# Router logits in column halves, weight splits in half-size pieces moved into the expert loop, and 24 unread TensorE products ahead of the attention

## The reference

```python
x = x + 0.5 * _L0_ffn_ref(_layernorm(x), router_w, w1, v1, w2)
x = x + _L0_attn_ref(_layernorm(x), Wq, bq, Wk, bk, Wv, bv, Wo, bo)
x = x + 0.5 * _L0_ffn_ref(_layernorm(x), router_w, w1, v1, w2)
```

## Time and profile before

| | us |
|---|---|
| median of 3 runs | 712.66 (712.17 to 713.16) |
| the profiled execution | 714.14 |
| span, first to last instruction, of that execution | 712.3 |
| busy: PE / PEld / DVE / ACT / POOL | 624.0 / 525.3 / 518.4 / 373.0 / 52.6 |
| mean granted TensorE clock | 0.950 of full |

### The profile page before, as it was taken

One profiled execution on the slowest core, in us unless ns is written; L12 is line 12 of the kernel. 1 busy time (PEld: TensorE's weight loads), 2 busy tenths in 40 slices (PEclk: granted clock), 3 DMA queues, 4 the chain that ended last, 5 costly groups with the idle time before them and its releaser, 6 DMA issues.

```text
span 712.3 us, 11934 instructions
## 1 busy us (share of the span) xinstructions
PE 624.0 (88%) x4498; PEld 525.3 (74%) x4498; DVE 518.4 (73%) x1308; ACT 373.0 (52%) x1001; POOL 52.6 (7%) x55
## 2 busy tenths in 40 slices
PE   3627985899999999999999999999999998663996
PEld 1414764699998979999897999898899996331775
DVE  6773656889987777878777777876878776865543
ACT  1403453576656656666555656565556665231432
POOL 3134300000000000000000000000000000115310
PEclk9956996999999999999999999999999999896999
DMA  8994970000000000000000000000000052793481
GB/s 328 407 351 153 373 277 1 0 1 1 1 1 2 1 1 1 1 1 1 1 1 1 1 1 1 1 1 0 1 1 1 1 204 93 311 397 87 156 300 46
DMA packets 27229, 62.50 MB, mean 88 GB/s; under 512 B 6880, under 2 KB 17248, under 8 KB 26912
## 3 DMA queue, kind: packets, MB, share of 16 engines
q1 hardware_dynamic: 25152, 56.05, 20.8%
q0 software_dynamic: 1568, 5.25, 2.2%
q10 hardware_dynamic: 448, 0.39, 0.2%
HBM read 54.34 MB, written 7.34 MB: 87 GB/s over the span
## 4 chain that ended last, share of the span: by engine, by line
PE 80%; DVE 11%; ACT 5%; DMA 2%; issue 1%; POOL 0%; SPq 0%; DVEq 0%; ACTq 0%
PE bank L1183 19%; PE bank L1185 18%; PE bank L1184 18%; PE bank L1235 8%; PE bank L1042 4%; PE bank L1074 4%; PE bank L1084 2%; PE bank L1117 2%; PE bank L1013 2%; DVE best L773 1%; DVE ln L695 1%; DMA slots<-token_table,slot_index 1%; PE bank L1026 1%; DVE keys L775 1%; DVE stats L683 1%
## 5 line engine op out<-in xcount | busy, mean ns | idle before, releaser
L609 ACT ACTIVATE probs<-bank,negmax 128x256 f32<-128x256 f32 x256 | 121.4, 494 | 0.0
L622 ACT CAST probsT_hi<-bank 128x512 fp32r<-128x512 f32 x128 | 68.8, 590 | 79.7 <-PE bank L1235 79.7
L957 DVE TENSOR_TENSOR probsT_lo<-bank,probsT_hi 128x512 fp32r<-128x512 f32 x128 | 81.8, 681 | 0.8 <-ACT probsT_hi L622 0.8
L925 DVE TENSOR_REDUCE negmax<-bank 128x2 f32<-128x512 f32 x128 | 81.8, 680 | 0.5 <-PE bank L1185 0.5
L592 ACT ACTIVATE o_hi<-bank,bv 128x512 fp32r<-128x512 f32 x64 | 44.2, 690 | 64.6 <-PE bank L1185 64.6
L1183 PE MATMUL bank<-k_hi,q_hi 128*128 128x256 f32 x256 | 72.5, 283 | 2.7 <-DVE q_lo L911 2.7
L933 DVE TENSOR_SCALAR probs<-probs,rowinv 128x256 f32<-128x256 f32 x256 | 73.1, 349 | 2.3
L1183 PE MATMUL bank<-o_hi,wo_hi 128*128 128x256 f32 x256 | 73.1, 286 | 1.6 <-DVE o_lo L911 1.6
L911 DVE SCALAR_TENSOR_TENSOR o_lo<-bank,bv,o_hi 128x512 fp32r<-128x512 f32 x64 | 48.0, 750 | 36.1 <-ACT o_hi L592 36.1
L1185 PE MATMUL bank<-o_hi,wo_lo 128*128 128x256 f32 x256 | 72.5, 283 | 0.0
L1185 PE MATMUL bank<-k_hi,q_lo 128*128 128x256 f32 x256 | 72.4, 283 | 0.0
(11 more groups left out here) (162 smaller groups left out, 1321.7 us busy)
## 6 DMA issues: line engine op xcount, KB each, us to landing
up_r<-up_in SPq DMA_DIRECT2D x16, 768.0 KB, 8.9
down_r<-down_in SPq DMA_DIRECT2D x14, 512.0 KB, 10.4
up_q<-up_in SPq DMA_DIRECT2D x8, 768.0 KB, 8.8
up_o<-up_in SPq DMA_DIRECT2D x6, 768.0 KB, 12.6
down_q<-down_in SPq DMA_DIRECT2D x8, 512.0 KB, 9.9
token_table<-xn SPq DMA_DIRECT2D x16, 256.0 KB, 10.7
down_o<-down_in SPq DMA_DIRECT2D x6, 512.0 KB, 14.2
x<-x_in SPq DMA_DIRECT2D x4, 512.0 KB, 5.4
```

The lines of the kernel that those rows point to most:

```text
L609: nc.scalar.activation(probs[:, n % 2, t, :], scores_ps[head][:, qt * S:qt * S + S], ACT.Exp, bias=negmax[:, n % 2, t:t + 1], accum_out=ro ...
L622: nc.scalar.copy(probsT[0][:, head].rearrange("p c s -> p (c s)"), probsT_ps[head][:]).then_inc(probsT_high, 1)
L925: nc.vector.reduce_max(negmax[:, n % 2, 2 * head:2 * head + 2], scores_ps[head][:].rearrange("p (t s) -> p t s", t=2), AX.X, negate=True). ...
L957: nc.vector.tensor_tensor(probsT[1][:, head].rearrange("p c s -> p (c s)"), probsT_ps[head][:], probsT[0][:, head].rearrange("p c s -> p ( ...
```

## The change

The router's product of four tiles is written as four products of 64 output rows and 256 columns, in which the two pairs of tiles use the two column halves of the array (`experts_of`); its result is 128 rows by 256 columns, so that it is copied and transposed back in two pieces instead of four. PE transposes up to three pairs ahead. At the start all 16 tiles are normalised together. The moment chain is grouped in 13 levels, within which operations don't wait for each other. The splits become 20 pieces of 512 columns; six of them move into steps 9 to 15 of layer 0's slot loop. SP holds the loads of groups 8 to 11 until three gathers have landed. The means of the first tiles are read from PSUM, and ACT does all four copies into `x`. In layer 1 POOL makes its keys after the last normalised tile. Two small stores at the end move from ACT's queue to POOL's, and one wide store from SP's to ACT's. PE runs 20 float32 products of 128 columns after layer 0's last sums, and 4 after the first transposes of the attention.

```diff
@@ sync: loads and stores @@
-            for g in range(6, 10):
+            for g in range(6, 8):
                 load(0, g)
             store_weights()
-            for g in range(10, AHEAD):
+            for n in range(3):
+                sp.wait_ge(gathered[n], 16)
+            for g in range(8, AHEAD):
                 load(0, g)
...
@@ gpsimd @@
             def expert_layer(layer):
+                if layer == 1:
+                    pool.wait_ge(xn_ready, 2 * TILES)
...
             expert_layer(1)
+            pool.wait_ge(staged[2], 1)
+            for j in range(2, 4):
+                store_narrow(nc.gpsimd, j, narrow_stored)
+            pool.wait_ge(narrow_stored, 32)
@@ scalar @@
+                if layer == 0 and SPLIT_AT <= s < SPLIT_AT + V_SPLIT:
+                    split_high(s - SPLIT_AT)
...
+                for u in range(3):
+                    copy_tokens(u)
+                for n in range(3):
+                    copy_expert_major(n)
+                    copy_tokens(2 * n + 3)
+                    if n > 0:
+                        copy_logits(n - 1)
+                    if n < 2:
+                        copy_tokens(2 * n + 4)
+                copy_expert_major(3)
+                copy_logits(2)
                 copy_logits(3)
...
-            for n in range(2):
+            for n, seen in ((1, (bank_summed, 2)), (0, (first_sums_read, 1))):
+                act.wait_ge(*seen)
+                for odd in range(2):
+                    nc.scalar.copy(rows_of_bank(n, odd), bank[6 + n][WIDE * odd:WIDE * odd + WIDE, :].rearrange(
+                        "p (b d) -> p b d", b=2)).then_inc(x_final, 1)
+            for n in range(6, 8):
                 split_high(n)
-            act.wait_ge(bank_summed, 2)
...
             warm(ACT.Exp)
-            split_high(3)
+            for n in range(8, 12):
+                split_high(n)
             act.wait_ge(bq_scaled, 1)
@@ vector @@
+                def level(*ops):
+                    dve.wait_ge(link, linked.now())
+                    for op, *args in ops:
+                        last = op(*args)
+                    last.then_inc(link, 1)
+                    linked.add()
...
+                    if layer == 0 and SPLIT_AT < s <= SPLIT_AT + V_SPLIT:
+                        split_low(s - SPLIT_AT - 1)
...
-                    split_low(0)
                     dve.wait_ge(bank_summed, 1)
                     for odd in range(2):
-                        nc.vector.tensor_copy(x[0:WIDE, 2 * odd, :], bank[6][WIDE * odd:WIDE * odd + WIDE, 0:D]).then_inc(x_final, 1)
+                        last = nc.vector.bn_stats(stats[0:WIDE, 2 * odd, :], bank[6][WIDE * odd:WIDE * odd + WIDE, 0:D])
+                    last.then_inc(first_sums_read, 1)
...
-            for n in range(2):
-                for m in range(2):
-                    dve.wait_ge(x_loaded[2 * n + m], 16)
-                    last = spread(range(8 * n + 4 * m, 8 * n + 4 * m + 4))
-                tie(last)
-                moments(8 * n, 8 * n + 8)
-                normalise(8 * n, 8 * n + 8)
+            for n in range(4):
+                dve.wait_ge(x_loaded[n], 16)
+                last = spread(range(4 * n, 4 * n + 4))
+            tie(last)
+            moments(0, TILES)
+            normalise(0, TILES)
...
+            in_fill = {2: 6, 3: 7, 5: 8, 7: 9}
+            in_step = {n: [lambda n=n: split_low(n + 9)] for n in range(1, 9)}
+            for n in range(2, 7):
+                in_step[n].append(lambda n=n: spread_first(2 * n))
+            in_step[7].append(lambda: tie(spread_first(14)))
+            in_step[8] += late_moments[:6]
+            in_step.update({9: late_moments[6:], 10: [lambda: split_low(18)], 11: [lambda: split_low(19)]})
@@ tensor @@
+            def keep_busy(count):
+                for _ in range(count):
+                    mm(bank[3][:, 0:KD * E], ident[:], router_w[:].rearrange("p k e -> p (k e)"),
+                       start=True, stop=True)
...
+                def experts_of(n):
+
+                    pe.wait_ge(xnT_ready, 8 * layer + 2 * n + 2)
+                    for kd in range(KD):
+                        for pair in range(2):
+                            last = mm(bank[3 + n % 2][E * pair:E * pair + E, 0:2 * P], router_w[:, kd, :],
+                                      xnT[:, (2 * n + pair) % 4, :, kd, :], start=kd == 0, stop=kd == KD - 1,
+                                      tile_position=(0, E * pair))
+                    last.then_inc(logitsT_raw, 1)
...
+                for u in range(3):
+                    transpose_tokens(u)
+                for n in range(4):
+                    experts_of(n)
+                    if n < 3:
+                        transpose_tokens(2 * n + 3)
+                    if n > 0:
+                        logits_of(n - 1)
+                    if n < 2:
+                        transpose_tokens(2 * n + 4)
                 logits_of(3)
...
+                if layer == 0:
+                    keep_busy(20)
                 pe.wait_ge(limit_ready, layer + 1)
...
             for n, job in enumerate(first_fills):
+                if n == KD:
+                    keep_busy(4)
```

More of the change, by code:

```diff
@@ L147, in macaron_kernel @@
                 exp8 = sb(router, "exp8", [P, TILES, 8])
-                key_i32 = sb(router, "key_i32", [P, T // 2], i32)
+                with ExitStack() as lent:
+                    sb(lent, "place_of_key_of_column", [P, T // 2])
+                    key_i32 = sb(lent, "key_i32", [P, T // 2], i32)
                 key_of_column = sb(router, "key_of_column", [P, T // 2])
@@ L426, in _ @@
             sp.wait_ge(staged[1], 1)
-            for odd in range(2):
-                store_wide(sp, 1, odd)
-            sp.wait_ge(out_stored, 16 * 10)
+            store_wide(sp, 1, 0)
+            sp.wait_ge(out_stored, 16 * 8)
         @block.gpsimd
@@ L559, in expert_layer @@
                         store_wide(nc.scalar, 0, odd)
-                    act.wait_ge(staged[2], 1)
-                    for j in range(2, 4):
-                        store_narrow(nc.scalar, j)
+                    act.wait_ge(staged[1], 1)
+                    store_wide(nc.scalar, 1, 1)
             def split_high(n):
@@ L650, in _ @@
                 for n in range(1, STEPS + 1):
-                    if i == 0 and n + 5 < len(splits):
-                        split_high(n + 5)
+                    if i == 0 and n + 11 < len(splits):
+                        split_high(n + 11)
                     step(n)
@@ L849, in late_range @@
                 dve.wait_ge(late_added[layer], r + 1)
-                if layer == 0 and r > 1:
-                    spread(range(1, TILES, 2))
+                if layer == 0:
+                    for a in range(0, TILES, 2):
+                        last = nc.vector.bn_stats(stats[WIDE:P, a, :], x[WIDE:P, a, :]) if r == 1 else spread([a + 1])
+                    last.then_inc(late_spread, 1)
+                    dve.wait_ge(late_spread, r)
             def split_low(n):
@@ L983, in _ @@
                     normalise_probs(0)
-                if between:
-                    between.pop(0)()
+                if n in in_fill:
+                    split_low(in_fill[n])
             step(0)
```

144 lines of the change are left out of this document (54 added, 90 removed).

## The result

The changed kernel takes 707.55 us in the median of 5 executions (705.54 to 710.26); the kernel before takes 712.85 beside it (712.17 to 714.06). The ratio is 0.9924, 95% interval 0.9907 to 0.9941: faster by 0.8%, but by 5.3 us and not by 17.7. The profiled execution is the slowest of the five: 710.26, span 708.4, which is 3.9 under the span before.

The account below looks back on a forecast made before the run. TensorE at full speed bounds the attention's middle; gains lie where it waits, in routers, gathers and the passage. Terms -2.7 - 4.85 + 0.3 - 5.05 + 0.4 - 5.2 - 0.6 = -17.7 gave 695.0 us, range 691 to 700.5.

Parts of the forecast that it names:

- Layer 0's router: Start of layer 0: with column halves side by side, POOL's subtraction starts earlier than its old 32.60; -2.7 us.
- rival 4: Routers of both layers: the product's halves don't run side by side, layer 0 gains nothing; 698 us, chance 8%.
- Layer 0's gather: Layer 0, slot numbers to first slots: weights' store lands early and no loads run beside the gather; -4.85 us.
- the slot loop: Layer 0's slots: the splits moved there are covered by engine gaps by less than 0.1 a slot; +0.3 us.
- Rival 6: Layer 0's slots: SP's hold makes weights late for ScalarE's split, so the kernel is slower; 716 us, chance 2%.
- The passage: Layer 0's last sums to the attention's second scores: earlier first fill (-2.35) and later gains (2.7); -5.05 us in all.
- rival 3: Passage to the attention: unread products stand in the way or the clock falls anyway; 698 to 699 us, chance 13%.
- First block: Attention's first block: VectorE ends 1.4 late in step 9, against TensorE slack of about 1; +0.4 us.
- Layer 1: Layer 1's router and gather: slot numbers 6.1 earlier, but the gather waits for the weights' store near 644.2; -5.2 us.
- Layer 1's slots: Layer 1, from first slots to the last stage copy: no change forecast, 0 us.
- The end: Last stores: all of SP's and ACT's issued by 709.1, POOL's two end no later; -0.6 us.
- Rival 2: Gathers of both layers gain only half, held by descriptors rather than loads; 700 us, chance 13%.

Follow-up runs that it names:

- e1: The changed kernel with SP holding layer 0's loads 8 to 11 for the first gather only, not three: 706.23 us, ratio 0.9922 to the kernel before.
- e5: The changed kernel with wq's later columns (1.5 of 2 MB) loaded behind group 15: 703.83 us, ratio 0.9872 to the kernel before.
- e4: The changed kernel without the 20 unread products after layer 0's last sums: 705.69 us, ratio 0.9904 to the kernel before.
- e10: The combined kernel e9 without the 20 unread products: 700.39 us, ratio 0.9821 to the kernel before.
- e3: The changed kernel with the end's narrow stores back on ACT's queue and the last wide one on SP's: 705.06 us, ratio 0.9877 to the kernel before.
- e9: The changed kernel with the edits of e5, e8 and e3 together: 699.94 us, ratio 0.9826 to the kernel before.
- e7: The changed kernel with layer 1's loads of groups 8 to 11 behind the token and weight stores, without a hold: 707.26 us, ratio 0.9934 to the kernel before.
- e8: The changed kernel with layer 1's loads of groups 8 to 11 behind the stores and held for three gathers: 704.27 us, ratio 0.9879 to the kernel before.

## Why the prediction was wrong, step by step

**Layer 0's router: right.** -2.99 at POOL's start, -2.7 forecast; rival 4 is out.

**Layer 0's gather: right at its place, and lost behind it.** First slots -7.83 for -7.55. The step that failed is the end of that paragraph and of the next: "four groups at 3.2 us each have landed by 66; group 8 is wanted near 73", and +0.3 for the slot loop. I followed the held groups and the weights of the splits, and stopped there; behind them in the same queue stand groups 12 to 15. By the forecast's own numbers: groups 8 to 15 are 10.4 MB, wk, wq and wv 3.1, the gathers' 1.7 go beside them, 15.2 in all; at 0.41 MB/us these are 37 us from 52.6, so nothing for slot 15 before 90, and near 95 if wo's 2 MB, issued at 82, share the rate. Slot 15 wanted them at 91.3 (99.13 - 7.83) and got them at 95.6. The trace of before could have told it: the same load landed at 99.1 there for products at 99.13. Even groups 8 to 11 had landed only by 71.9 instead of 66 (the last issued at 56.09, with 15.8 to landing), since gathers and wk shared the rate. Rival 6 had the right cause (SP's hold makes weights late) and looked at the wrong weights; its slack of 7 to 11 was 1 to 2 as well (wk landed at 73.4 for a split at 75.08, wq at 79.3 for one at 80.37). The splits themselves cost nothing: the slots keep their period of 2.65 up to slot 11, behind which the waits begin, and in e1 up to slot 14. e5 took 1.5 MB out of the queue and got 3.0 of the 4.0 back; e1 shows that an earlier start doesn't help, since it slows the slots that release the later loads.

**The clock in the sums: not foreseen.** +2.47 in the profile. It stood in three of the seven profiles with long waits in slot 15 and in none of the seven with short ones, so the waits seem to be needed for it, but they are not enough. It is a matter of the profiled execution, and the medians hold it in part at most.

**The passage: mechanism right, size near.** Where the clock held, sums to first fill take 9.26 to 9.70 (forecast 9.0, before 11.33) and from there to the second scores 15.25 to 15.28 (14.9, before 17.58): -4.0 to -4.4 of -5.05. In the changed kernel's profile the clock fell ahead of the transposes and stayed down through them (rival 3), -3.3. That the clock stays because "TensorE idles 2.0 at most" was wrong: it idled 2.48 and the clock fell. *The Trainium skill ("TensorE: Matmul & The Clock Gate", "Part 4: PE-mode transpose") says that the full clock does not engage for transposes, which do not count as busy in the same way. These profiles can't confirm it: in four of the six falls the clock was down before the first transpose, and in five of the eleven profiles with the products it stayed at full through the transposes.* The bound was not ScalarE either: `xT_hi` waits 0.3 to 1.2 for TensorE's transposes in every profile of the changed kernels. The products' price is at my lower bound. They had no use that the medians can tell (e4, e10).

**First block:** +0.6 to +0.7 where no clock falls (474.94 to 475.07 against 474.36), forecast 0.4. The other 1.6 are the clock's fall behind the second scores.

**Layer 1: -3.98 for -5.2.** The first tiles were as forecast (eight in 2.68) and the bound was named rightly: the weights' store landing behind the loads. I set it at 644.2 with attention ending at its old time. With attention's end 2.1 earlier that is 642.1; the store landed at 642.7 and the gather started at 643.4. So 0.6 of the miss is a later landing, and 0.7 is the step from the landing to the gather's start, which the forecast left out; layer 0 of the kernel before has the same step (landing at 50.7, gather at 51.51). *The Trainium skill ("SBUF — State Buffer", "Who interferes with whom") has the port pair as an exclusive lock. The trace agrees: in the kernel before two of the eight tiles took 0.91 and 1.18, ending right behind POOL's key-making instructions, and the other six 0.40 each; eight tiles take 2.68 again once the key making is out of the way.*

**Layer 1's slots: +0.50, forecast 0.** No edit touches them, and this stage takes 53.7 to 55.0 in the other profiles, so it is spread.

**The end: wrong sign.** I said "POOL's two end no later". Their data do not, but POOL's drain of 2.93 behind them does: +1.70, and e3 gives back 2.5 in the medians and 1.80 in the stage (7.13 to 5.33). *The Trainium skill ("DMA: Bandwidth & Descriptors", "SWDGE vs HWDGE vs iDMA") would have plain transfers on SP's and ACT's queues; the trace agrees with 5.33 against 7.13.*

Rival 2 (gathers gain half) did not happen in either layer. The profile fell short by 13.8. The largest part is that the sum had no term for a load that is late: 4.1, and 6.5 with the clock behind it. The rest is 2.3 at the end, 1.8 in the first block, 1.7 in the passage, 1.2 and 0.5 in layer 1, less 0.3 gained in layer 0's first stage. So the late loads alone don't explain the miss of the range: without them (e5) the median is 703.83, still above it. With wq's later columns moved, the end's stores moved back and layer 1 held as layer 0 (e9), the span is 14.1 under before's, of which 2.7 is layer 1's hold, which the change did not have.

## What to carry to other kernels

When a load is held back, follow its queue to its end: add up all bytes that still have to land before the last consumer and divide by the rate. Look in the profile before for the hole that the queue loses, and for how long before its use each load lands: here the last one had no slack to begin with. Order what stands in a full queue by who waits first; here 1.5 MB that nobody needed yet cost 3.7 us. Leave the last stores of a kernel to the queues of SP and ACT: on POOL's, its drain (2.9 us here) stands at the end.

## What the runs showed of the hardware

- The TensorE clock falls behind the same gap in some profiled executions and not in others: waits of 2.7 us, five of eleven, one for each kernel. Profiled once, such a kernel may be read 1.6 to 5 us too slow (an estimate from what the falls cost); the changed kernel's profiled execution had all three falls.
- Under the 20 unread products the clock stood at 1.00 from 104 on, where it had been at 0.50 under the sums, TensorE being busy in both; it was down again 2.2 us after they ended (at 108.6), while TensorE idled.
- POOL's drain took 2.93 us behind its two stores in all eight profiles that have them, and its last 2 us stand alone: all data had landed about 2 us ahead of the end.
- A gather beside a full load queue takes 6.0 to its first slots, 3.05 without; behind a store that lands late it waits as long. It is one price, paid at either place (e7, e8).
